# Attention stage of a transformer layer: all four row scalings on VectorE, and two constant loads issued later

## The chip, the cores and the metric

The kernel runs on one Trainium2 chip with all 8 cores, each core on its own eighth of the rows, with no exchange between cores. The metric is the device time in microseconds (us) of the slowest core; the program is one launch.

## The reference

One transformer layer on a sequence of 8192 rows of width 2048, with an unusual attention: for every row, the 16 heads attend to each other, so each softmax is over 16 numbers.

```python
x = x + attn(layernorm(x), w_qkv, w_proj)      # x: 1 x 8192 x 2048
x = x + ffn(layernorm(x), kernel, bias)

def attn(x, w_qkv, w_proj):                    # N_HEAD 16, HEAD_DIM 128
    qkv = (x @ w_qkv.T).reshape(B, N, 3, 16, 128)
    q, k, v = qkv[:, :, 0], qkv[:, :, 1], qkv[:, :, 2]
    att = softmax(einsum('bnid,bnjd->bnij', q, k) * 128 ** -0.5)
    out = einsum('bnij,bnjd->bnid', att, v)    # 16 x 16 per row
    return out.transpose(0, 2, 1, 3).reshape(B, N, 2048) @ w_proj.T

def ffn(x, kernel, bias):                      # 8-bit fake quantization of x, kernel, bias and result
    return fake_quant(relu(fake_quant(x) @ fake_quant(kernel) + fake_quant(bias)))
```

## The kernel before, in words

The kernel is written with raw engine queues: every engine has its own program, runs it strictly in order, and waits on counting semaphores (`wait_ge`) that instructions of other engines raise (`inc`). There is no scheduler; the order in the source is the order on the engine. A core has 1024 rows, and works in stages.

- Stage A: 8 tiles of 128 rows. SyncE (SP) loads `xbuf` (two buffers, 1 MB each; the load of tile t waits for tile t-2), VectorE takes the statistics, ScalarE normalizes into `abuf`, TensorE transposes it with the identity matrix `ident` into PSUM `pH`, ScalarE copies it to `aT`. TensorE's first transpose waits for the semaphore `aCn`, which the loads of `ident` and `mask4` raise. Meanwhile GpSimd (POOL) loads the first three slabs `wqb` of the QKV weights with a cast.
- Stage B: the QKV product, 48 slabs, which leaves `qT`, `kT` and `vT`.
- Stage C: attention, a loop over g of NG = 32 groups. One group is four 128x128 blocks, each of 8 rows times 16 heads, so that a block of q times k holds 8 wanted 16x16 squares on its diagonal; the mask `mask4` keeps those.
- Stage D: the output projection (`wpb` times `sT`), with the residual `xr` and, between its tiles, the quantized FFN weights (`ktb`, `kqb`, `qk`). Then the FFN with its quantization steps, the bias, and the stores.

One pass g of the stage C loop, in the order of each engine's queue (all buffers are in pairs, `g % 2`; k = g - 1):

- TensorE: transpose of v(g) (L317), q times k (g) (L324), transpose of the normalized weights `Abuf`(k) into `pH` (L335), product with v (k) (L344). In short: V(g), QK(g), AT(k), MM(k).
- ScalarE: exponential of group g into `Ebuf` (L358), scaling of blocks 2 and 3 of group g into `Abuf` (L366), copy of the transposed weights `aTTbuf`(k) out of PSUM (L378), copy of the result into `sT` (k) (L383). In short: Exp(g), scale(g), aTT(k), sT(k).
- VectorE: copy of transposed v into `V8buf`(g) (L395), mask (L398), row sums (L401), reciprocal (L405), scaling of blocks 0 and 1 of group g into `Abuf` (L410).
- GpSimd loads one of 16 slabs `wpb` of the projection weights every second pass (L426), into the space that v(g) has left; SyncE loads six of the eight `xr` tiles at the stage's start and two at its end.

The semaphores that matter: `cA8` (QK done), `cExp` (Exp done), `cRcp` (reciprocal done), `cAsc` and `cAsS` (VectorE's and ScalarE's share of the scaling done), `cAtT` (AT done), `cT1e` (aTT done), `cO8` (MM done). A pass g of ScalarE waits for `cA8` of g before Exp, for `cRcp` of g before its scaling, for `cAtT` of k before aTT, and for `cO8` of k before sT.

Of the kernel before, what the change touches and what calls it, by code (L numbers as in the profile page):

```python
# [10 lines left out]
AF = mybir.ActivationFunctionType  # L11
# [15 lines left out]
def build_program():  # L27
# [65 lines left out]
    def S_(name):  # L93
        if name not in sems:
            sems[name] = nc.semaphore(name).__enter__()
            cnt[name] = 0
        return sems[name]

    def inc(instr, name, k=1):
        h = S_(name)  # L100
        instr.then_inc(h, k)
        cnt[name] += k
        return (name, cnt[name])
# [13 lines left out]
    with nc.Block() as blk:  # L117
# [31 lines left out]

        @blk.sync  # L150
        def _(sync):
            inc(sync.dma_start(ident[:, :], d_ident[:, :]), "aCn", 16)
            inc(sync.dma_start(mask4[:, :], d_mask[:, :]), "aCn", 16)
            for t in range(NT):
                if t >= 2:
                    sync.wait_ge(S_("aVn"), t - 1)
                    sync.wait_ge(S_("aVv"), t - 1)
                inc(sync.dma_start(xbuf[t % 2][:, :],
                                   d_xatt[128 * t:128 * (t + 1), :]),
                    f"aLd{t % 2}", 16)  # L160
            for idx in range(2 * NC):
                ft, hh = idx // 2, idx % 2
                if idx >= 2:
                    sync.wait_ge(S_("fK1"), idx - 1)
                inc(sync.dma_start(ktc[idx % 2][:, :],
                                   d_wkT[128 * ft:128 * (ft + 1),
                                         1024 * hh:1024 * (hh + 1)]),
                    f"fKt1{idx % 2}", 16)
# [134 lines left out]
    if PHASES >= 3:  # L303
# [3 lines left out]
     with nc.Block() as blk:  # L307
        @blk.tensor
        def _(tn):
            for g in range(NG + 1):  # L310
                if g < NG:
                    m, cg = g // 2, g % 2
                    if g >= 2:
                        tn.wait_ge(S_("cV8e"), g - 1)
                    for j in range(4):
                        sl = slab(m, 4 * cg + j)
                        tr = tn.transpose(pH[2 + g % 2][:, 128 * j:128 * (j + 1)],  # L317
                                          vT[:, sl:sl + 128], ident[:, :])
                    inc(tr, "cV8t")
                    if g >= 2:  # L320
                        tn.wait_ge(S_("cExp"), g - 1)
                    for j in range(4):
                        sl = slab(m, 4 * cg + j)
                        mm = tn.matmul(pF[g % 2][:, 128 * j:128 * (j + 1)],  # L324
                                       qT[:, sl:sl + 128], kT[:, sl:sl + 128],
                                       start=True, stop=True)
                    inc(mm, "cA8")
                k = g - 1
                if k >= 0:
                    tn.wait_ge(S_("cAsc"), k + 1)  # L330
                    tn.wait_ge(S_("cAsS"), k + 1)
                    if k >= 2:
                        tn.wait_ge(S_("cT1e"), k - 1)
                    for j in range(4):
                        tr = tn.transpose(pH[k % 2][:, 128 * j:128 * (j + 1)],  # L335
                                          Abuf[k % 2][:, 128 * j:128 * (j + 1)],
                                          ident[:, :])
                    inc(tr, "cAtT")
                    tn.wait_ge(S_("cT1e"), k + 1)
                    tn.wait_ge(S_("cV8e"), k + 1)  # L340
                    if k >= 2:
                        tn.wait_ge(S_("cO8e"), k - 1)
                    for j in range(4):
                        mm = tn.matmul(pF[2 + k % 2][:, 128 * j:128 * (j + 1)],  # L344
                                       V8buf[k % 2][:, 128 * j:128 * (j + 1)],
                                       aTTbuf[k % 2][:, 128 * j:128 * (j + 1)],
                                       start=True, stop=True)
                    inc(mm, "cO8")

        @blk.scalar  # L350
        def _(s):
            s.wait_ge(S_("aC12"), 1)
            for g in range(NG + 1):
                if g < NG:
                    s.wait_ge(S_("cA8"), g + 1)
                    if g >= 2:
                        s.wait_ge(S_("cAsc"), g - 1)
                    inc(s.activation(Ebuf[g % 2][:, :], pF[g % 2][:, :], AF.Exp,  # L358
                                     bias=col(80), scale=SCALE), "cExp")

                if g < NG:
                    s.wait_ge(S_("cRcp"), g + 1)
                    if g >= 2:
                        s.wait_ge(S_("cAtT"), g - 1)
                    for j in range(2, 4):
                        instr = s.activation(Abuf[g % 2][:, 128 * j:128 * (j + 1)],  # L366
                                             Embuf[g % 2][:, 128 * j:128 * (j + 1)],
                                             AF.Copy,
                                             scale=C_R4(g % 2)[:, j:j + 1])
                        if j < 3:  # L370
                            inc(instr, "selfS")
                    inc(instr, "cAsS")
                k = g - 1
                if k >= 0:
                    s.wait_ge(S_("cAtT"), k + 1)
                    if k >= 2:
                        s.wait_ge(S_("cO8"), k - 1)
                    inc(s.copy(aTTbuf[k % 2][:, :], pH[k % 2][:, :]), "cT1e")  # L378
                    s.wait_ge(S_("cO8"), k + 1)
                    km, kc = k // 2, k % 2  # L380
                    dst = sT.rearrange("p (t x) -> p t x", t=8)[
                        :, 4 * kc:4 * kc + 4, 128 * km:128 * (km + 1)]
                    inc(s.copy(  # L383
                        dst, pF[2 + k % 2][:, :].rearrange("p (j l) -> p j l", j=4)),
                        "cO8e")

        @blk.vector
        def _(v):
            for g in range(NG + 1):
                if g < NG:  # L390
# [11 lines left out]
                        C_S4(p), Embuf[p][:, :].rearrange("p (b n) -> p b n", b=4),  # L402
                        AX.X), "selfV")
                    wt(v, h_rs)
                    h_rc = inc(v.reciprocal(C_R4(p), C_S4(p)), "cRcp")  # L405
                    if g >= 2:
                        v.wait_ge(S_("cAtT"), g - 1)
                    wt(v, h_rc)
                    for j in range(2):
                        instr = v.tensor_scalar(Abuf[p][:, 128 * j:128 * (j + 1)],  # L410
                                                Embuf[p][:, 128 * j:128 * (j + 1)],
                                                C_R4(p)[:, j:j + 1], None, ALU.mult)
                        if j < 1:
                            inc(instr, "selfV")
                    inc(instr, "cAsc")

# [548 lines left out]
```

## Time and profile before

| | us |
|---|---|
| median of 2 timed runs | 974.39 (973.4 to 975.38) |
| the profiled execution's own time | 972.12 |
| span of its slowest core (core 2), first to last instruction | 970.6 |
| spans of the eight cores | 963.6 to 970.6 |
| mean granted TensorE clock, all cores | 0.842 to 0.845 of full speed |
| TensorE busy, slowest core | 680.5 (70%) |
| VectorE busy | 556.9 (57%) |
| ScalarE busy | 342.9 (35%) |
| stage C, from its first matmul to its last copy (core 2) | 411.46 to 591.17 |

The span is the stretch from the first to the last instruction of a core, so a point in the trace is given in us from its start. The granted clock has two levels, full (1.00, 2.4 GHz) and half (0.50, 1.2 GHz); a mean between them is a mixture in time. Busy shares are over the whole span and mix stages with different limits.

### The profile page before, as it was taken

How to read it: one execution, taken by the hardware profiler on the slowest of the kernel's cores; microseconds unless marked ns; L12 is line 12 of the kernel's file. 1: busy time of each engine (PE TensorE's matmuls, PEld its weight loads, DVE VectorE, ACT ScalarE, POOL GpSimd, SP SyncE). 2: the span in 40 equal slices, each digit the busy share in tenths (PEclk: the TensorE clock that was granted, in tenths of full speed). 3: DMA queues.
4: the chain of work that ended last, by engine and by line, in shares of the span. 5: the costliest groups of instructions: out<-in, count | busy, mean ns of one | idle time of the engine just before them, and what ended most of it. 6: DMA issues, size and time to landing. Idle time of an engine off the chain costs nothing.

```text
span 970.6 us, 11061 instructions; the slowest of 8 cores (963.6 to 970.6 us)
## 1 busy us (share of the span) xinstructions
PE 680.5 (70%) x3524; PEld 341.7 (35%) x3584; DVE 556.9 (57%) x885; ACT 342.9 (35%) x427; POOL 111.0 (11%) x93
## 2 busy tenths in 40 slices
PE   1157999999999999823333335995596645978790
PEld 1033444444444444423223222452052322434340
DVE  2352445454545453443433432898188897899997
ACT  3365434343434343444444441321021233243220
POOL 1000111111111111000000000001200000111324
PEclk9997999999999999955555556997598877999896
DMA  9454799999999978291111114447912210111122
GB/s 163 126 174 43 74 109 146 159 143 153 150 145 162 155 88 81 22 282 23 27 28 23 22 23 141 133 128 176 150 66 88 79 52 1 44 44 44 44 87 87
DMA packets 116985, 94.21 MB, mean 97 GB/s; under 512 B 101184, under 2 KB 101312, under 8 KB 113856
## 3 DMA queue, kind: packets, MB, share of 16 engines
q0 software_dynamic: 103680, 33.56, 34.4%
q1 hardware_dynamic: 13248, 59.94, 18.5%
q8 instruction: 30, 0.49, 0.2%
q14 instruction: 27, 0.22, 0.1%
HBM read 118.65 MB, written 8.39 MB: 131 GB/s over the span
## 4 chain that ended last, share of the span: by engine, by line
DVE 25%; issue 11%; PE 9%; ACT 6%; DMA 5%; DVEq 1%; ACTq 0%; POOLq 0%; POOL 0%; SPq 0%
DMA wpb<-wpT 3%; PE pF L550 3%; DVE cols L401 2%; ACT Ebuf L358 2%; DVE bnbuf L603 2%; PE pF L344 2%; DVE ktb L700 2%; DVE cols L668 2%; DVE xr L569 2%; DVE kti L704 2%; ACT aTTbuf L378 2%; DMA ktb<-wkT 2%; DVE ttile L811 2%; ACT Abuf L366 1%; DVE Embuf L398 1%
## 5 line engine op out<-in xcount | busy, mean ns | idle before, releaser
L288 PE MATMUL pF<-aT,wqb 128*128 128x512 bf16 x736 | 278.9, 379 | 1.6
L286 PE MATMUL pF<-aT,wqb 128*128 128x512 bf16 x706 | 267.6, 379 | 1.0 <-DMA wqb<-wqkvT 1.0
L550 PE MATMUL pF<-qk,xqs 128*128 128x512 bf16 x500 | 116.3, 392 | 4.8 <-ACT xqs L897 3.9
L514 PE MATMUL pF<-wpb,sT 128*128 128x512 bf16 x240 | 99.0, 412 | 22.5 <-DMA wpb<-wpT 20.7
L517 PE MATMUL pF<-wpb,sT 128*128 128x512 bf16 x256 | 105.8, 413 | 4.1 <-DMA wpb<-wpT 1.9
L286 PEld LDWEIGHTS pF<-aT,wqb 128*128 128x128 bf16 x736 | 72.0, 98 | 88.2 <-issue 1.5
L288 PEld LDWEIGHTS pF<-aT,wqb 128*128 128x128 bf16 x736 | 72.0, 98 | 86.7
L344 PE MATMUL pF<-aTTbuf,V8buf 128*128 128x128 bf16 x128 | 18.7, 301 | 115.7 <-ACT aTTbuf L378 115.7
L301 POOL DMA_DIRECT2D wqb<-wqkvT x48 | 55.0, 1146 | 333.9 <-PE pF L288 243.0
L113 DVE CAST qT<-pF 128x512 bf16<-128x512 f32 x16 | 42.9, 2682 | 65.0 <-PE pF L288 50.0
L113 DVE CAST vT<-pF 128x512 bf16<-128x512 f32 x16 | 42.6, 2661 | 58.8 <-PE pF L288 58.8
L550 PEld LDWEIGHTS pF<-qk,xqs 128*128 128x128 bf16 x512 | 51.4, 101 | 67.1 <-issue 11.9
L113 DVE CAST kT<-pF 128x512 bf16<-128x512 f32 x16 | 43.0, 2687 | 50.2 <-PE pF L288 50.2
L114 ACT COPY qk<-pH 128x512 bf16<-128x512 bf16 x64 | 33.5, 592 | 101.9 <-PE pH L493 101.9
L114 ACT CAST kT<-pF 128x512 bf16<-128x512 f32 x16 | 43.2, 2703 | 68.5 <-PE pF L288 68.5
L114 ACT CAST qT<-pF 128x512 bf16<-128x512 f32 x16 | 43.3, 2708 | 66.3 <-PE pF L288 58.7
L114 ACT CAST vT<-pF 128x512 bf16<-128x512 f32 x16 | 42.8, 2672 | 67.7 <-PE pF L288 67.7
L437 POOL TENSOR_TENSOR xr<-xr,junkG 128x2048 f32<-128x2048 f32 x7 | 33.3, 4750 | 223.8 <-DVE junkG L837 223.8
L344 PEld LDWEIGHTS pF<-aTTbuf,V8buf 128*128 128x128 bf16 x128 | 11.2, 127 | 123.2 <-issue 123.2
L395 DVE COPY V8buf<-pH 128x512 bf16<-128x512 bf16 x32 | 13.6, 425 | 70.7 <-PE pH L317 70.7
L266 PE MATMUL pH<-ident,abuf 128*128 128x128 bf16 x128 | 15.2, 290 | 55.3 <-ACT aT L114 36.6
L514 PEld LDWEIGHTS pF<-wpb,sT 128*128 128x128 bf16 x256 | 26.3, 103 | 69.6 <-issue 45.5
(117 smaller groups left out, 875.9 us busy)
## 6 DMA issues: line engine op xcount, KB each, us to landing
wqb<-wqkvT POOLq DMA_DIRECT2D x48, 512.0 KB, 8.0
ktc<-wkT SPq DMA_DIRECT2D x32, 512.0 KB, 7.1
ktb<-wkT SPq DMA_DIRECT2D x32, 512.0 KB, 4.0
xbuf<-x_att SPq DMA_DIRECT2D x8, 1024.0 KB, 7.1
xr<-x_res SPq DMA_DIRECT2D x8, 1024.0 KB, 6.7
wpb<-wpT POOLq DMA_DIRECT2D x32, 256.0 KB, 5.5
out<-xr SPq DMA_DIRECT2D x7, 1024.0 KB, 3.8
bias_b<-bias SPq DMA_DIRECT2D x1, 1024.0 KB, 4.2
```

Of the source, the lines that this page charges most:

```text
L113: return eng.tensor_copy(dst, srcap)
L114: return eng.copy(dst, srcap)
L286: tn.matmul(pa[:, :], wch, aT[:, 1024 * c:1024 * c + 512], start=st, stop=sp)
L288: mm = tn.matmul(pb[:, :], wch, aT[:, 1024 * c + 512:1024 * c + 1024], start=st, stop=sp)
L301: inc(g.dma_start(dst, src), f"bWq{e % 3}", 16)
L344: mm = tn.matmul(pF[2 + k % 2][:, 128 * j:128 * (j + 1)], V8buf[k % 2][:, 128 * j:128 * (j + 1)], aTTbuf[k % 2][:, 128 * j:128 * (j + 1)], ...
L358: inc(s.activation(Ebuf[g % 2][:, :], pF[g % 2][:, :], AF.Exp, bias=col(80), scale=SCALE), "cExp")
L378: inc(s.copy(aTTbuf[k % 2][:, :], pH[k % 2][:, :]), "cT1e")
L437: inc(g.tensor_tensor(xr[:, 2048 * k:2048 * (k + 1)], xr[:, 2048 * k:2048 * (k + 1)], junkG2[:, :], ALU.add), "gOutR")
L514: tn.matmul(pF[2 * (idx % 2)][:, :], lhs, wpb[:, 1024 * m:1024 * m + 512], start=st, stop=sp)
L517: mm = tn.matmul(pF[2 * (idx % 2) + 1][:, :], lhs, wpb[:, 1024 * m + 512:1024 * (m + 1)], start=st, stop=sp)
L550: mm = tn.matmul(pF[u][:, :], xqs[Mt % 2][:, 128 * c:128 * (c + 1)], qk[:, 2048 * c + 512 * u:2048 * c + 512 * (u + 1)], start=(c == 0), s ...
```

## The change

Two edits. In stage C, ScalarE no longer scales blocks 2 and 3; VectorE scales all four, the semaphore `cAsS` is gone, and the reciprocal no longer raises `cRcp` for ScalarE. In stage A, the loads of `ident` and `mask4` are issued on SyncE behind the first two `xbuf` loads instead of ahead of them.

```diff
--- before.py
+++ after.py
@@ -149,9 +149,10 @@
 
         @blk.sync
         def _(sync):
-            inc(sync.dma_start(ident[:, :], d_ident[:, :]), "aCn", 16)
-            inc(sync.dma_start(mask4[:, :], d_mask[:, :]), "aCn", 16)
             for t in range(NT):
+                if t == 2:
+                    inc(sync.dma_start(ident[:, :], d_ident[:, :]), "aCn", 16)
+                    inc(sync.dma_start(mask4[:, :], d_mask[:, :]), "aCn", 16)
                 if t >= 2:
                     sync.wait_ge(S_("aVn"), t - 1)
                     sync.wait_ge(S_("aVv"), t - 1)
@@ -328,7 +329,6 @@
                 k = g - 1
                 if k >= 0:
                     tn.wait_ge(S_("cAsc"), k + 1)
-                    tn.wait_ge(S_("cAsS"), k + 1)
                     if k >= 2:
                         tn.wait_ge(S_("cT1e"), k - 1)
                     for j in range(4):
@@ -358,18 +358,6 @@
                     inc(s.activation(Ebuf[g % 2][:, :], pF[g % 2][:, :], AF.Exp,
                                      bias=col(80), scale=SCALE), "cExp")
 
-                if g < NG:
-                    s.wait_ge(S_("cRcp"), g + 1)
-                    if g >= 2:
-                        s.wait_ge(S_("cAtT"), g - 1)
-                    for j in range(2, 4):
-                        instr = s.activation(Abuf[g % 2][:, 128 * j:128 * (j + 1)],
-                                             Embuf[g % 2][:, 128 * j:128 * (j + 1)],
-                                             AF.Copy,
-                                             scale=C_R4(g % 2)[:, j:j + 1])
-                        if j < 3:
-                            inc(instr, "selfS")
-                    inc(instr, "cAsS")
                 k = g - 1
                 if k >= 0:
                     s.wait_ge(S_("cAtT"), k + 1)
@@ -402,15 +390,15 @@
                         C_S4(p), Embuf[p][:, :].rearrange("p (b n) -> p b n", b=4),
                         AX.X), "selfV")
                     wt(v, h_rs)
-                    h_rc = inc(v.reciprocal(C_R4(p), C_S4(p)), "cRcp")
+                    h_rc = inc(v.reciprocal(C_R4(p), C_S4(p)), "selfV")
                     if g >= 2:
                         v.wait_ge(S_("cAtT"), g - 1)
                     wt(v, h_rc)
-                    for j in range(2):
+                    for j in range(4):
                         instr = v.tensor_scalar(Abuf[p][:, 128 * j:128 * (j + 1)],
                                                 Embuf[p][:, 128 * j:128 * (j + 1)],
                                                 C_R4(p)[:, j:j + 1], None, ALU.mult)
-                        if j < 1:
+                        if j < 3:
                             inc(instr, "selfV")
                     inc(instr, "cAsc")
 
```

How it stands in the queues. ScalarE in the stage C loop, one pass and the start of the next, before (`Ebuf`, `Abuf`, `aTTbuf` as above, the number behind a name tells the two buffers apart):

```order
L358 ACTIVATE Ebuf_71<-pF,cols 128x512 [waits cA8,cAsc]
L366 ACTIVATE Abuf_75<-Embuf_73,cols 128x128 [waits cRcp,cAtT]
L366 ACTIVATE Abuf_75<-Embuf_73,cols 128x128
L378 COPY aTTbuf_76<-pH 128x512 [waits cAtT,cO8]
L383 CAST sT<-pF 128x4x128 [waits cO8]
L358 ACTIVATE Ebuf_70<-pF,cols 128x512 [waits cA8,cAsc]
```

and after (behind the removed block the line numbers of the changed file are lower by 12):

```order
L371 CAST sT<-pF 128x4x128 [waits cO8]
L358 ACTIVATE Ebuf_71<-pF,cols 128x512 [waits cA8,cAsc]
L366 COPY aTTbuf_76<-pH 128x512 [waits cAtT,cO8]
L371 CAST sT<-pF 128x4x128 [waits cO8]
L358 ACTIVATE Ebuf_70<-pF,cols 128x512 [waits cA8,cAsc]
```

The copy aTT(k) now follows Exp(g) directly, and ScalarE's queue has no wait for a result of VectorE's pass g.

VectorE in the same loop, before:

```order
L395 COPY V8buf_78<-pH 128x512 [waits cV8t,cO8]
L398 TENSOR_TENSOR Embuf_72<-Ebuf_70,mask_90 128x512 [waits cExp]
L401 TENSOR_REDUCE cols<-Embuf_72 128x4 [waits selfV]
L405 RECIPROCAL cols<-cols 128x4 [waits selfV]
L410 TENSOR_SCALAR Abuf_74<-Embuf_72,cols 128x128 [waits cAtT,cRcp]
L410 TENSOR_SCALAR Abuf_74<-Embuf_72,cols 128x128
```

and after:

```order
L383 COPY V8buf_78<-pH 128x512 [waits cV8t,cO8]
L386 TENSOR_TENSOR Embuf_72<-Ebuf_70,mask_90 128x512 [waits cExp]
L389 TENSOR_REDUCE cols<-Embuf_72 128x4 [waits selfV]
L393 RECIPROCAL cols<-cols 128x4 [waits selfV]
L398 TENSOR_SCALAR Abuf_74<-Embuf_72,cols 128x128 [waits cAtT,selfV]
L398 TENSOR_SCALAR Abuf_74<-Embuf_72,cols 128x128 x3
```

Two scalings of 128x128 have become four; nothing else is reordered on VectorE.

## Rows read from the trace of the kernel before

**Rows 1.** The chain that ended last, 405 to 600 us, shares by line.

```profile
by line: issue 17.2%; DVE cols L401 11.4%; ACT Ebuf L358 11.4%; PE pF L344 9.6%; ACT aTTbuf L378 7.9%; ACT Abuf L366 7.3%; DVE Embuf L398 7.2%; PE pF L324 6.9%; PE pH L317 6.8%; DMA ktb<-wkT 5.6%; DVE cols L405 3.1%; DVEq L106 0.7%; ACT L35
```

**Rows 2.** Timeline of a stage C pass: start us, us, engine, line, [idle before <-releaser].

```profile
565.26 0.58 PE L344 MATMUL pF<-aTTbuf,V8buf 128*128 128x128 bf16 x4 [3.68 <-ACT aTTbuf L378]
...
565.64 0.63 PE L317 MATMUL pH<-ident,vT 128*128 128x128 bf16 x4
...
566.06 0.63 PE L324 MATMUL pF<-kT,qT 128*128 128x128 bf16 x4
...
566.49 0.63 PE L335 MATMUL pH<-ident,Abuf 128*128 128x128 bf16 x4
566.85 0.69 ACT L358 ACTIVATE Ebuf<-pF,cols 128x512 bf16<-128x512 f32 x1 [0.33 <-PE pF L324]
567.64 0.42 DVE L398 TENSOR_TENSOR Embuf<-Ebuf,mask 128x512 bf16<-128x512 bf16 x1 [0.77 <-ACT Ebuf L358]
568.17 0.69 DVE L401 TENSOR_REDUCE cols<-Embuf 128x4 f32<-128x512 bf16 x1
568.96 0.18 DVE L405 RECIPROCAL cols<-cols 128x4 f32<-128x4 f32 x1
569.24 0.42 DVE L410 TENSOR_SCALAR Abuf<-Embuf,cols 128x128 bf16<-128x128 bf16 x2
569.28 0.69 ACT L366 ACTIVATE Abuf<-Embuf,cols 128x128 bf16<-128x128 bf16 x2 [1.75 <-DVE cols L405]
569.88 0.56 ACT L378 COPY aTTbuf<-pH 128x512 bf16<-128x512 bf16 x1
...
570.80 0.58 PE L344 MATMUL pF<-aTTbuf,V8buf 128*128 128x128 bf16 x4 [3.68 <-ACT aTTbuf L378]
```

**Rows 3.** Windows view, 29 passes from Exp(2) to Exp(31).

```profile
core 2: us, PE busy (x) PEld busy (x) DVE busy (x) ACT busy (x) POOL busy (x), PEclk, DMA share, GB/s
421.80:583.84 162.04, 54.10 (x467) 47.23 (x465) 61.82 (x175) 70.65 (x146) 7.41 (x14) 0.50 0.22 49
```

**Rows 4.** Tile view of Abuf, VectorE's scalings: min/median/max ns.

```profile
L410 DVE TENSOR_SCALAR Abuf<-Embuf,cols x64: 246/252/255, 415.8 to 586.4; 128x128 bf16<-128x128 bf16 x64
```

**Rows 5.** Timeline of the end of stage C.

```profile
583.84 0.69 ACT L358 ACTIVATE Ebuf<-pF,cols 128x512 bf16<-128x512 f32 x1 [0.33 <-PE pF L324]
...
588.17 0.63 PE L335 MATMUL pH<-ident,Abuf 128*128 128x128 bf16 x4
...
588.95 0.59 ACT L378 COPY aTTbuf<-pH 128x512 bf16<-128x512 bf16 x1
...
590.58 0.59 ACT L383 CAST sT<-pF 128x512 bf16<-128x512 f32 x1 [1.03 <-PE pF L344]
```

**Rows 6.** Timeline of the start of stage C.

```profile
411.46 0.38 PE L317 MATMUL pH<-ident,vT 128*128 128x128 bf16 x4 [3.07 <-PEq L117]
...
411.68 0.39 PE L324 MATMUL pF<-kT,qT 128*128 128x128 bf16 x4
...
413.45 0.69 ACT L358 ACTIVATE Ebuf<-pF,cols 128x512 bf16<-128x512 f32 x1
```

**Rows 7.** Timeline, GpSimd's last slab load of stage C.

```profile
583.86 0.53 POOL L426 DMA_DIRECT2D wpb<-wpT  x1 [10.92 <-PE pH L317]
```

**Rows 8.** Page, DMA issues: count, KB each, median us to landing.

```profile
wpb<-wpT POOLq DMA_DIRECT2D x32, 256.0 KB, 5.5
```

**Rows 9.** Windows view of TensorE alone: length, busy (count), granted clock, DMA share, GB/s.

```profile
692.00:698.00 6.00, 3.67 (x7) 0.50 1.05 173
```

**Rows 10.** Timeline of stage A: first loads, first transposes, third tile's statistics.

```profile
1.07 0.38 SPq L152 DMA_DIRECT2D ident<-ident  x1
...
1.98 59.07 SPq L158 DMA_DIRECT2D xbuf<-x_att  x8
...
18.72 1.87 PE L266 MATMUL pH<-ident,abuf 128*128 128x128 bf16 x16 [18.72 <-ACT abuf L196]
...
34.08 2.47 DVE L211 BATCH_NORM_STATS2 bnbuf<-xbuf 128x6 f32<-128x512 f32 x4 [16.17 <-DMA xbuf<-x_att]
```

## The prediction

> **What bounds the kernel now.** I read the chain that ended last first. Over the attention stage it runs through every engine in turn: exponential, row sums, product with v, transposed copy, scaling, mask [rows 1]. No engine is full there: in 162.04 us TensorE is busy 54.10, VectorE 61.82, ScalarE 70.65 [rows 3]. So the stage is bound by waiting, and I read one pass of the timeline [rows 2]. In it I call the pass's group g and the one before it k.
>
> The pass is one closed ring. Exp(g) starts at 566.85. The mask follows at 567.64 (+0.79), the row sums at 568.17 (+0.53), the reciprocal at 568.96 (+0.79). ScalarE's scaling starts at 569.28 (+0.32). The copy aTT(k) starts at 569.88 (+0.60), and MM(k) at 570.80 (+0.92). From MM to the next transpose of v is 0.38, from there to QK 0.42, from QK to Exp 0.79 (565.26, 565.64, 566.06, 566.85). The sum is 5.54, the period of an undisturbed pass [rows 2]. The 29 passes from 421.80 to 583.84 average 5.59, so some are late, by 1.4 us together [rows 3].
>
> What the reader is to see is the place of aTT(k). Its input comes from AT(k), which starts at 566.49 and takes 0.63, so it is there before 567.2. Its engine is idle: ScalarE waits 1.75 us for the reciprocal ahead of its scaling [rows 2]. The copy of the old group stands in ScalarE's queue behind the scaling of the new one, and so TensorE's MM(k), idle for 3.68, and everything behind MM(k), hangs on the softmax of g. The ring closes once a pass although the buffers are in pairs.
>
> **The change part by part.** *ScalarE's queue.* Two scalings leave it (0.69 us for both, 569.28), and with them its wait for the reciprocal. aTT(k) now stands right behind Exp(g). Two rings are left, and the longer one sets the period.
>
> Ring one closes in one pass: Exp(g), aTT(k) 0.60 later (the 0.69 of Exp less the overlap seen between 569.28 and 569.88), MM(k) +0.92, V +0.38, QK +0.42, Exp +0.79: 3.11 us.
>
> Ring two goes through the softmax and closes in two passes, because AT(g) and MM(g) stand one pass later in TensorE's queue, ahead of QK(g+2): Exp(g) to mask 0.79, sums 0.53, reciprocal 0.79, VectorE's scaling 0.28 (568.96 to 569.24), four scalings, hand-over to AT(g), AT to aTT 0.78 (588.17 to 588.95 [rows 5]), MM 0.92, V 0.38, QK 0.42, Exp 0.79. All but two terms are rows.
>
> *The four scalings.* Two take 0.42 together [rows 2] and one 0.252 [rows 4], so each further one adds 0.17, and four take 0.42 + 0.34 = 0.76. If they did not overlap it would be 1.01. I take 0.76, since the row with two shows the overlap.
>
> There the Trainium skill speaks against the change: "VectorE: DVE Perf Modes", § The DRAIN you can't avoid, has the next VectorE operation start only when the pipe is empty. By it the four would take 1.01, which is 0.125 us more a pass. The row with two in 0.42 [rows 2] disagrees, and I stay with it.
>
> *The hand-over from VectorE to TensorE* isn't in the trace as a wait that ends last. The nearest rows are QK's end at 566.06 + 0.63 = 566.69 to Exp at 566.85, which is 0.16 with two semaphores waited for, as AT now has; below, 0.11 inside VectorE (567.64 + 0.42 to 568.17); above, 0.36 from the copy's end to MM (569.88 + 0.56 to 570.80) with three semaphores [rows 2]. I take 0.16, the nearest in kind, and keep 0.11 and 0.36.
>
> Ring two: 0.79 + 0.53 + 0.79 + 0.28 + 0.76 + 0.16 + 0.78 + 0.92 + 0.38 + 0.42 + 0.79 = 6.60 for two passes, 3.30 a pass. It is the longer one. VectorE's own work is no ring above it: 61.82 / 29 = 2.13 a pass now, 2.47 with two more scalings, and gaps of 0.10 between dependent instructions bring it to about 2.7. ScalarE's is 0.69 + 0.56 + 0.59 = 1.84.
>
> *The stage.* Exp(0) starts at 413.45, after a table load that stays [rows 6]. Exp(1) is free at once. Exp(2) needs one round of ring two: 413.45 + 6.60 = 420.05. Exp(31) is 29 passes later: + 95.7 = 515.75. From there to the end: 0.79 + 0.53 + 0.79 + 0.28 + 0.76 + 0.16 + 0.78 = 4.09 to the last aTT, and from it to the end of the last copy what the trace has, 588.95 to 591.17, 2.22 [rows 5]. End at 522.06 in place of 591.17: 69.1 saved. The late passes' 1.4 us may stay: 67.7.
>
> *What starts earlier.* GpSimd loads a slab every second pass, then every 6.6 us, against 5.5 to landing [rows 8]. The last one is issued at 583.86, as Exp(31) starts, and would land 5.5 later, 0.8 us before the new stage's end (6.31 after Exp(31)); the projection uses it as the last of its sixteen slabs. Nothing is late. The other loads at the stage's end and all behind them hang on the stage's own last copy and move with it, so I book the whole gain.
>
> *The two constant loads.* The first `xbuf` load is issued 0.91 us earlier (1.98 against 1.07) [rows 10]. `ident` and `mask4` come behind 2 MB, but TensorE needs them only at 18.72. If they are later, the price is small up to 34.08, when the third tile arrives and ends a wait of 16.17 [rows 10]: the first two tiles' transposes have that gap as cover, and beyond it each us costs one. That third load is issued when tile 0 is normalized, so it can gain up to 0.9, or nothing if the traffic of GpSimd's three slabs sets its landing. The bounds are a gain of 0.9 and a loss of 2; I take a gain of 0.5.
>
> *The sum.* 67.7 + 0.5 = 68.2 off the profiled execution's 972.12 gives 903.9. That execution is 2.3 below the median of the timed runs, 974.39; off the median it gives 906.2.
>
> **The rivals.**
>
> *TensorE's clock rises in the stage.* It runs at half speed, 0.50, through all of it [rows 3]. At full speed four matmuls take 0.39 in place of 0.63 and the next group follows after 0.22 in place of 0.42 [rows 6, 2]. Ring two has QK to Exp and AT to aTT (0.24 less each), V to QK (0.20) and MM to V (0.16) in it: 5.76, or 2.88 a pass, 12.2 us less over 29 passes, 0.84 in the first round and 0.4 in the tail. The projection behind it would open at full speed; I allow up to 3 for that, which no row here prices. 16 in all: 890. For it: TensorE's busy share goes from 54.10 / 162.04 to about 1.87 / 3.30, 57%. Against it: the stretch at 692 has it busy 3.67 of 6 us, 61%, and stays at 0.50 [rows 9]. The Trainium skill ("TensorE: Matmul & The Clock Gate", § What's actually happening) says that the default is the throttled state and that activity releases it; which side 57% in short bursts falls on, no row settles.
>
> *VectorE becomes uneven.* Its work goes from 38% to some 75% of a pass, and GpSimd issues its loads beside it. With scalings that don't overlap (+0.125 a pass), a hand-over of 0.36 (+0.10) and GpSimd's 16 issues of 0.53 [rows 7] each holding VectorE on the ring (8.5 us), it is 31 x 0.225 = 7.0 and 8.5, 15 more: 921. For it: 1.4 us of late passes exist now [rows 3], and my ring has no slack in VectorE. "SBUF — State Buffer", § Who interferes with whom, in the Trainium skill, lets a GpSimd access and a VectorE operation in a two-port mode block each other, whichever comes first. The trace agrees at most to the size of those 1.4 us.
>
> *The change does not do what it says*: something else that I overlooked holds aTT(k) or MM(k) until pass g is through, and the period stays near 5.5. Against it: the queue behind Exp(g) holds only waits for `cAtT` and `cO8`, both long met. 972.
>
> *Slower.* One mechanism: the scalings on VectorE, now with nothing between them, each cost far more than alone. VectorE's own pass of about 2.7 us would then become the bound. To reach the old 5.59 both added ones must cost 1.45 more, some 1.6 each; a loss of 2% (19.5 us, 0.6 a pass) needs 1.9 each, in place of 0.17: 994. The 64 scalings now lie between 0.246 and 0.255 [rows 4].
>
> **How the numbers follow.** The forecast at the half clock: 66%, 906, by itself 901 to 914. The clock rises, wholly or in parts: 18%, 888 to 900. VectorE uneven: 13%, 914 to 922. No effect: 2%. Slower: 1%. The range of 8 in 10 has to take in most of the second and third: 888 to 920. A measurement of this kernel can tell 2% (19.5 us) from no change; all three leading cases are beyond it: faster 0.97, the same 0.02, slower 0.01.
>
> **What would show it.** In the changed kernel's trace: Exp to Exp in pairs that average 3.30; aTT(k) starting behind Exp(g) or 0.78 behind AT(k), not behind the reciprocal; TensorE's wait ahead of MM(k) down from 3.68 to about 1; four scalings in 0.76; the clock at 0.50; the stage from 411 to 522; the stages behind it with their old lengths. I am wrong if the period lies outside 3.1 to 3.6, if the clock rises, or if a later stage takes back what this one gives, a wait for slabs first of all.

## The result, and the profile after

The changed kernel takes 909.53 us (median of 9 runs) where the kernel before, timed beside it, takes 975.42 (8 runs). The ratio is 0.932, with a 95% interval of 0.9297 to 0.9343: 6.8% faster. The forecast was 906, the range 888 to 920. The profiled execution took 905.0 us in all; its slowest core is core 6 with a span of 903.5. The runs of this kernel spread from 905.0 to 912.2 us, apart from one disturbed execution (974.91, with four cores at a lower clock), which the median of 9 holds (it is 909.25 without it) and the ratio leaves out, as do the times, ratios and profiles of the experiments below with theirs.

First the place. The table has medians over the eight cores of each kernel's profiled execution: the first statistics of stage A (start of the first L211), the first matmul of stage B's main loop (L286), stage C from the start of its first matmul (L317) to the end of its last copy (L383), and from there to the end of the core's span (line numbers of the kernel before).

| us | before | after |
|---|---|---|
| first statistics of stage A | 9.4 | 7.2 |
| main loop of stage B begins | 87.0 | 86.7 |
| stage C begins | 408.0 | 407.6 |
| stage C, length | 180.1 | 112.5 |
| end of stage C to end of span | 378.8 | 379.2 |

Stage C gives 67.6 us, and nothing behind it takes that back or adds to it. The first statistics of stage A come 2.2 us earlier; at the later boundaries the lead is 0.3 or 0.4, which is no more than the difference between two kernels that are alike up to there (stage B begins at 87.0 before, and at 86.5 with the scaling edit alone).

The timeline of one double pass of stage C after the change, core 6 (start us, us, engine, line, [idle before <-releaser]); it answers to [rows 2]. Lines from the removed block on are lower by 12 than before: the copy aTT is now L366, the row sums L389, the scalings L398. Between the moved loads and AT they are higher by one (V is L318, QK L325); AT, MM and Exp keep L335, L344 and L358.

```profile
462.72 0.69 ACT L358 ACTIVATE Ebuf<-pF,cols 128x512 bf16<-128x512 f32 x1 [0.33 <-PE pF L325]
463.31 0.59 ACT L366 COPY aTTbuf<-pH 128x512 bf16<-128x512 bf16 x1
463.51 0.43 DVE L386 TENSOR_TENSOR Embuf<-Ebuf,mask 128x512 bf16<-128x512 bf16 x1 [0.77 <-ACT Ebuf L358]
464.04 0.69 DVE L389 TENSOR_REDUCE cols<-Embuf 128x4 f32<-128x512 bf16 x1
...
464.25 0.58 PE L344 MATMUL pF<-aTTbuf,V8buf 128*128 128x128 bf16 x4 [1.09 <-ACT aTTbuf L366]
...
464.83 0.18 DVE L393 RECIPROCAL cols<-cols 128x4 f32<-128x4 f32 x1
...
465.12 0.74 DVE L398 TENSOR_SCALAR Abuf<-Embuf,cols 128x128 bf16<-128x128 bf16 x4
...
465.84 0.69 ACT L358 ACTIVATE Ebuf<-pF,cols 128x512 bf16<-128x512 f32 x1 [0.33 <-PE pF L325]
...
466.11 0.58 PE L335 MATMUL pH<-ident,Abuf 128*128 128x128 bf16 x4 [0.42 <-DVE Abuf L398]
...
466.84 0.59 ACT L366 COPY aTTbuf<-pH 128x512 bf16<-128x512 bf16 x1 [0.31 <-PE pH L335]
...
467.78 0.59 PE L344 MATMUL pF<-aTTbuf,V8buf 128*128 128x128 bf16 x4 [1.09 <-ACT aTTbuf L366]
...
469.38 0.69 ACT L358 ACTIVATE Ebuf<-pF,cols 128x512 bf16<-128x512 f32 x1 [0.33 <-PE pF L325]
```

What to see: the copy aTT(k) (463.31) starts 0.59 us behind Exp (462.72), with no wait; before, it stood 3.03 us behind (566.85 to 569.88 [rows 2]). The next Exp comes 3.12 us after the first, the one after that 3.54 later (465.84, 469.38). This alternation is the mark of a ring that closes once in two passes: the softmax of the group that begins at 462.72 runs through mask, sums, reciprocal and four scalings to AT at 466.11, aTT at 466.84 and MM at 467.78, and only from there to the Exp at 469.38, that is 6.66 us in all. The MM at 464.25 between them belongs to the group before. The four scalings take 0.74 together (465.12), so they overlap as two did.

The windows view of the 29 passes from Exp(2) to Exp(31), which answers to [rows 3]:

```profile
core 6: us, PE busy (x) PEld busy (x) DVE busy (x) ACT busy (x) POOL busy (x), PEclk, DMA share, GB/s
422.34:519.90 97.56, 58.19 (x465) 44.69 (x464) 69.63 (x233) 52.80 (x88) 7.44 (x14) 0.50 0.40 83
```

97.56 us in place of 162.04, 3.36 a pass in place of 5.59. VectorE is now busy for 69.63 of it, 71% in place of 38%; the clock is 0.50 as before.

The end of stage C, which answers to [rows 5] and [rows 7]:

```profile
519.90 0.69 ACT L358 ACTIVATE Ebuf<-pF,cols 128x512 bf16<-128x512 f32 x1 [0.33 <-PE pF L325]
519.92 0.53 POOL L414 DMA_DIRECT2D wpb<-wpT  x1 [6.12 <-PE pH L318]
...
524.02 0.59 ACT L366 COPY aTTbuf<-pH 128x512 bf16<-128x512 bf16 x1 [1.28 <-PE pH L335]
...
525.63 0.59 ACT L371 CAST sT<-pF 128x512 bf16<-128x512 f32 x1 [1.03 <-PE pF L344]
```

The last slab load is issued with the last Exp (519.92), 6.3 us before the stage ends (525.63 + 0.59 = 526.22). The tail from Exp(31) is 526.22 - 519.90 = 6.32; it was forecast as 6.31.

Stage A, which answers to [rows 10]:

```profile
1.07 0.85 SPq L159 DMA_DIRECT2D xbuf<-x_att  x2
...
1.96 0.42 SPq L154 DMA_DIRECT2D ident<-ident  x1
2.43 1.15 SPq L155 DMA_DIRECT2D mask<-mask  x1
8.20 2.47 DVE L212 BATCH_NORM_STATS2 bnbuf<-xbuf 128x6 f32<-128x512 f32 x4 [8.20 <-DMA xbuf<-x_att]
...
17.24 1.86 PE L267 MATMUL pH<-ident,abuf 128*128 128x128 bf16 x16 [17.24 <-ACT abuf L197]
...
32.59 2.47 DVE L212 BATCH_NORM_STATS2 bnbuf<-xbuf 128x6 f32<-128x512 f32 x4 [16.15 <-DMA xbuf<-x_att]
```

The first `xbuf` loads are issued at 1.07, and the first statistics start at 8.20 on this core. The constants behind them are there at 17.24, when TensorE has its first input; it waits for `abuf`, not for them. But the third tile comes at 32.59 where it came at 34.08 [rows 10], on the slowest cores of each; over eight cores the median lead is 2.2 us at the first tile, 0.7 at the third (33.2 and 32.5) and 0.4 where stage B begins, which is no longer more than two like kernels differ there.

### The profile page after: what moved, and what is told of

Read it like the earlier page. It is cut to its first block, busy times and chain, and to the rows that moved or that the text cites. A ratio compares the mean times of both kernels' runs of the same rounds, so it can differ in the third digit from the quotient of the medians.

```text
span 903.5 us, 11027 instructions; the slowest of 8 cores (896.3 to 903.5 us)
## 1 busy us (share of the span) xinstructions
PE 690.0 (76%) x3584; PEld 339.0 (38%) x3584; DVE 565.6 (63%) x949; ACT 323.0 (36%) x363; POOL 110.9 (12%) x93
## 4 chain that ended last, share of the span: by engine, by line
DVE 24%; PE 12%; issue 9%; DMA 5%; ACT 3%; DVEq 1%; POOLq 0%; POOL 0%; ACTq 0%; SPq 0%
DMA wpb<-wpT 4%; PE pF L502 3%; PE pF L505 3%; DVE bnbuf L591 2%; DVE cols L656 2%; DVE ttile L799 2%; PE pF L538 2%; DVE cols L802 2%; ACT Ebuf L358 1%; DVE cols L389 1%; DVE ktb L688 1%; DVE Abuf L398 1%; DVE xr L557 1%; ACT aTTbuf L366 1%; PE pF L344 1%
## 5 line engine op out<-in xcount | busy, mean ns | idle before, releaser
L287 PE MATMUL pF<-aT,wqb 128*128 128x512 bf16 x736 | 279.9, 380 | 3.1 <-DMA wqb<-wqkvT 3.1
L289 PE MATMUL pF<-aT,wqb 128*128 128x512 bf16 x736 | 280.0, 380 | 0.0
L502 PE MATMUL pF<-wpb,sT 128*128 128x512 bf16 x256 | 106.0, 414 | 24.0 <-DMA wpb<-wpT 21.8
L538 PE MATMUL pF<-qk,xqs 128*128 128x512 bf16 x512 | 117.7, 393 | 3.6 <-ACT xqs L885 3.6
L505 PE MATMUL pF<-wpb,sT 128*128 128x512 bf16 x256 | 106.2, 415 | 0.0
L425 POOL TENSOR_TENSOR xr<-xr,junkG 128x2048 f32<-128x2048 f32 x7 | 33.2, 4749 | 223.6 <-DVE junkG L825 223.6
L344 PE MATMUL pF<-aTTbuf,V8buf 128*128 128x128 bf16 x128 | 18.7, 301 | 35.5 <-ACT aTTbuf L366 35.5
L212 DVE BATCH_NORM_STATS2 bnbuf<-xbuf 128x6 f32<-128x512 f32 x32 | 19.8, 681 | 37.8 <-DMA xbuf<-x_att 37.8
L856 ACT CAST qx<-xi 128x2048 bf16<-128x2048 int32 x8 | 15.2, 1903 | 65.9 <-DVE xi L640 65.9
```

The source lines that it names most:

```text
L212: h_bn = inc(v.bn_stats(bnbuf[:, 6 * q4:6 * q4 + 6], xbt[:, 512 * q4:512 * (q4 + 1)]), "selfV")
L287: tn.matmul(pa[:, :], wch, aT[:, 1024 * c:1024 * c + 512], start=st, stop=sp)
L289: mm = tn.matmul(pb[:, :], wch, aT[:, 1024 * c + 512:1024 * c + 1024], start=st, stop=sp)
L344: mm = tn.matmul(pF[2 + k % 2][:, 128 * j:128 * (j + 1)], V8buf[k % 2][:, 128 * j:128 * (j + 1)], aTTbuf[k % 2][:, 128 * j:128 * (j + 1)], ...
L425: inc(g.tensor_tensor(xr[:, 2048 * k:2048 * (k + 1)], xr[:, 2048 * k:2048 * (k + 1)], junkG2[:, :], ALU.add), "gOutR")
L502: tn.matmul(pF[2 * (idx % 2)][:, :], lhs, wpb[:, 1024 * m:1024 * m + 512], start=st, stop=sp)
```

## The experiments

Ten kernels ran, each as a diff to the changed kernel or the kernel before. The ratio is to the kernel before on the same chip, with its 95% interval; period is the mean from Exp(2) to Exp(31), clock the granted clock in that stretch; all but the ratio are medians over the eight cores of the profiled execution.

| kernel | ratio | period | stage C | clock in C | end of C to end |
|---|---|---|---|---|---|
| before | 1 | 5.60 | 180.1 | 0.50 | 378.8 |
| changed | 0.932 (0.9297 to 0.9343) | 3.36 | 112.5 | 0.50 | 379.2 |
| scaling edit alone | 0.9292 (0.9267 to 0.9318) | 3.36 | 112.4 | 0.50 | 378.9 |
| constants edit alone | 0.9987 (0.9967 to 1.0007) | 5.60 | 180.1 | 0.50 | 379.1 |
| ScalarE scales, last in its queue | 0.9423 (0.94 to 0.9446) | 3.81 | 126.2 | 0.50 | 378.4 |
| ScalarE scales, between aTT and sT | 0.9324 (0.927 to 0.9377) | 3.55 | 117.7 | 0.50 | 379.5 |
| wait for the reciprocal kept | 0.9822 (0.9795 to 0.9848) | 5.03 | 162.5 | 0.50 | 379.1 |
| eight scalings | 0.9408 (0.9369 to 0.9446) | 3.69 | 122.9 | 0.50 | 379.1 |
| filler matmuls | 0.9162 (0.91 to 0.9225) | 2.92 | 99.2 | 0.98 | 377.8 |
| two groups deep | 0.9238 (0.9134 to 0.9342) | 3.11 | 103.6 | 0.50 | 378.7 |
| two deep and filler | 0.9064 (0.9019 to 0.9108) | 2.60 | 88.8 | 0.98 | 378.1 |
| those, and ScalarE shares, a group late | 0.9014 (0.8913 to 0.9114) | 2.54 | 85.9 | 0.97 | 378.7 |

The last column is the control: no edit of stage C changes what lies behind it by more than 1.4 us, and the eight cores of the changed kernel alone spread there from 377.2 to 381.5. So stage C's length can be read for each kernel without the noise of the whole time. It is the better measure here: most times of the experiments lie some us below expectations that were counted from the changed kernel's 909.5 (the scaling edit alone by 5, with the same stage C), and no run shows why. The ratios of the eight scalings, the filler, two deep, and both together rest on three runs of the kernel before, those of the two kernels with ScalarE between and a group late on four.

### The two edits apart

The scaling edit alone:

```diff
+            inc(sync.dma_start(ident[:, :], d_ident[:, :]), "aCn", 16)
+            inc(sync.dma_start(mask4[:, :], d_mask[:, :]), "aCn", 16)
             for t in range(NT):
-                if t == 2:
-                    inc(sync.dma_start(ident[:, :], d_ident[:, :]), "aCn", 16)
-                    inc(sync.dma_start(mask4[:, :], d_mask[:, :]), "aCn", 16)
```

> The changed kernel with the two constant loads put back ahead of the first xbuf load, so the scaling edit alone. Theory (the stage C ring carries the whole gain): stage C stays at 112.5 us against 180.1 before, and the time is that of the changed kernel, 909.5, plus 0 to 1 us. Rival (the earlier xbuf loads, which bring the first statistics forward by some 2 us, carry through to the end): 911 to 912.

The constants edit alone is the other half of the change's diff, on the kernel before.

> The kernel before with only the constant loads moved behind the first two xbuf loads. Theory: 0 to 0.9 us faster than 975.4, so not to be told from no change; the first statistics start 1 to 2 us earlier, and the start of stage B moves by less, since the third tile's landing is set by the traffic. Rival: the 2 us come through whole, 973.4, or the late constants hold up the transposes, over 976.

Measured: 904.12 us, ratio 0.9292, for the scaling edit; 972.67 against 973.65, ratio 0.9987 with 1 inside its interval, for the constants. The first interval overlaps that of the whole change, so the constants edit is worth nothing that these runs can tell, and the scaling edit has the whole gain. The time was expected as 909.5 to 910.5 and came out 5 lower; stage C (112.4) and what lies behind it (378.9) are as in the changed kernel, so the 5 do not come from there. With the constants edit the median first statistics start at 7.3 in place of 9.4, the third tile's at 32.4 in place of 33.2, and stage B at 86.4 in place of 87.0. The first part of the expectation holds: the lead is lost on the way to the third tile. That GpSimd's slab traffic is what it is lost to was only argued.

### Who scales, or where the copy stands

The rival reading of the gain is that ScalarE was relieved, or that VectorE is faster at scaling (0.74 for four against 0.69 for two). The first experiment leaves the work shared as before and only moves ScalarE's block of L361 to L372 in its queue, against the kernel before with the constants edit:

```diff
-                if g < NG:
-                    s.wait_ge(S_("cRcp"), g + 1)
...
-                    inc(instr, "cAsS")
                 k = g - 1
                 if k >= 0:
...
                         "cO8e")
+                if g < NG:
+                    s.wait_ge(S_("cRcp"), g + 1)
...
+                    inc(instr, "cAsS")
```

> ScalarE keeps its two scalings and VectorE its two, but ScalarE's queue has them behind aTT(k) and sT(k): Exp(g), aTT(k), sT(k), scale(g). Theory (the place of aTT(k) in the queue is what counts, not who scales): the two-pass ring is 0.60 + 0.92 + 0.68 + 0.50 + 0.69 + 0.16 + 0.78 + 0.92 + 0.38 + 0.42 + 0.79 = 6.84, 3.42 a pass, some 0.06 more with the late passes as in the changed kernel: stage C 116, time 913. Rival (the gain comes from taking work from ScalarE, or from VectorE's faster scalings): the period stays near 5.5 and the time near 975.

Measured: 917.28, stage C 126.2, a period of 3.81. The order of the queue alone brings 53.9 of the 67.6 us, so who scales is not the main thing. But 3.42 a pass was forecast, and that missed by 0.4. Its timeline (core 1):

```profile
440.76 0.70 ACT L380 ACTIVATE Abuf<-Embuf,cols 128x128 bf16<-128x128 bf16 x2
...
441.36 0.68 ACT L359 ACTIVATE Ebuf<-pF,cols 128x512 bf16<-128x512 f32 x1
...
441.71 0.59 PE L336 MATMUL pH<-ident,Abuf 128*128 128x128 bf16 x4 [0.67 <-ACT Abuf L380]
...
442.44 0.59 ACT L367 COPY aTTbuf<-pH 128x512 bf16<-128x512 bf16 x1 [0.40 <-PE pH L336]
...
443.38 0.59 PE L345 MATMUL pF<-aTTbuf,V8buf 128*128 128x128 bf16 x4 [1.09 <-ACT aTTbuf L367]
...
444.06 0.59 ACT L372 CAST sT<-pF 128x512 bf16<-128x512 f32 x1 [1.03 <-PE pF L345]
...
444.54 0.70 ACT L380 ACTIVATE Abuf<-Embuf,cols 128x128 bf16<-128x128 bf16 x2
```

There is a ring that I had left out. The scaling at 440.76 releases AT at 441.71 (+0.95), that the copy at 442.44 (+0.73), that MM at 443.38 (+0.94), that sT at 444.06 (+0.68), and the next scaling stands behind sT in the queue, at 444.54 (+0.48): 3.78 in one pass. The expectation had taken aTT(k) as ready whenever Exp was through; here it waits for AT(k), because the scaling that feeds AT(k) comes so late.

The next kernel opens that ring, with the scaling between aTT(k) and sT(k):

> As the run with ScalarE's two scalings last, but they stand between aTT(k) and sT(k): Exp(g), aTT(k), scale(g), sT(k). The run with them last had a period of 3.78, from a ring I had left out: scale(g) to AT(g) 0.95, to aTT(g) 0.73, to MM(g) 0.94, to sT(g) 0.68, to scale(g+1) 0.48. Theory (that ring, closed by sT standing ahead of the scaling): here it opens, and the longest is Exp(g) through the softmax to scale(g), sT(k), Exp(g+1): 0.79 + 0.53 + 0.79 + 0.32 + 0.60 + 0.50 = 3.53 a pass, stage C 118 to 120, time 909 to 911. Rival (two engines sharing the scaling cost the 0.4 a pass by themselves): 3.8, 917.

Measured: 910.63, stage C 117.7, and passes of 3.50 each but for a few late ones, mean 3.55; forecast 3.53. The two kernels differ in one place of the queue and share the work alike, so the revised account holds and its rival falls. In time this one can't be told from the changed kernel (0.9324 and 0.932); stage C is 5.2 us longer.

The opposite experiment has VectorE do all the scaling, and puts back only the wait:

```diff
+                if g < NG:
+                    s.wait_ge(S_("cRcp"), g + 1)
                 k = g - 1
                 if k >= 0:
                     s.wait_ge(S_("cAtT"), k + 1)
```

> VectorE scales all four blocks as in the changed kernel, but ScalarE still waits for the reciprocal of group g ahead of aTT(k). Theory: the one-pass ring is closed again, without the 0.60 of the two scalings: 0.79 + 0.53 + 0.79 + 0.32 + 0.92 + 0.38 + 0.42 + 0.79 = 4.94 a pass; 31 x (4.94 - 3.36) = 49 us more than the changed kernel, 958. Rival (who does the work is what counts): near 909.5.

Measured: 955.77, a period of 5.03, stage C 162.5, 49.9 longer than in the changed kernel. One wait with no work behind it takes back 74% of the gain. Core 5's timeline:

```profile
501.11 0.69 ACT L358 ACTIVATE Ebuf<-pF,cols 128x512 bf16<-128x512 f32 x1 [0.33 <-PE pF L325]
...
503.22 0.18 DVE L395 RECIPROCAL cols<-cols 128x4 f32<-128x4 f32 x1
...
503.60 0.59 ACT L368 COPY aTTbuf<-pH 128x512 bf16<-128x512 bf16 x1 [1.80 <-DVE cols L395]
...
504.54 0.59 PE L344 MATMUL pF<-aTTbuf,V8buf 128*128 128x128 bf16 x4 [3.15 <-ACT aTTbuf L368]
...
506.13 0.69 ACT L358 ACTIVATE Ebuf<-pF,cols 128x512 bf16<-128x512 f32 x1 [0.33 <-PE pF L325]
```

The copy (L368) starts 0.38 behind the reciprocal, with 1.80 us of idle ScalarE ahead of it, and Exp comes again after 5.02 us.

### How long the ring is, and how often it closes

Four more scalings on VectorE ahead of the four, into a buffer that nothing reads; the result is unchanged:

```diff
+                    for j in range(4):
+                        inc(v.tensor_scalar(kqb[0][:, 128 * j:128 * (j + 1)],
+                                            Embuf[p][:, 128 * j:128 * (j + 1)],
+                                            C_R4(p)[:, j:j + 1], None, ALU.mult), "selfV")
```

> The changed kernel with four more scalings of 128x128 on VectorE ahead of the four, into a buffer that nothing reads, 4 x 0.17 = 0.68 us a pass. Theory (they lie on a ring that closes once in two passes): half of it shows, 0.34 a pass, 31 x 0.34 = 10.5, time 920, as long as VectorE's own pass (some 2.7 + 0.68 = 3.4) stays under the period of 3.7. Rival (VectorE is the bound, or the ring closes once a pass): the whole 0.68 shows, 21 us, 931.

Measured: a period of 3.69, 0.33 above the changed kernel's 3.36. The timeline (core 1) shows the price of the four: 482.47 to 483.13 is 0.66, and half of that is 0.33. Stage C is 10.4 longer against 10.5 expected; the time is 917.09 against 920.

```profile
482.47 0.74 DVE L398 TENSOR_SCALAR kqb<-Embuf,cols 128x128 bf16<-128x128 bf16 x4
...
483.13 0.74 DVE L403 TENSOR_SCALAR Abuf<-Embuf,cols 128x128 bf16<-128x128 bf16 x4
...
483.78 0.42 DVE L383 COPY V8buf<-pH 128x512 bf16<-128x512 bf16 x1
...
484.12 0.58 PE L335 MATMUL pH<-ident,Abuf 128*128 128x128 bf16 x4 [0.53 <-DVE Abuf L403]
484.54 0.42 DVE L386 TENSOR_TENSOR Embuf<-Ebuf,mask 128x512 bf16<-128x512 bf16 x1 [0.34 <-ACT Ebuf L358]
```

Behind the scalings the copy V8 (483.78) follows at once, and the mask (484.54) still waits 0.34 for Exp: VectorE is nearly full here and still not the bound.

Two groups deep, in the loops of TensorE and ScalarE, so that the softmax has a pass more before AT(k):

```diff
-            for g in range(NG + 1):
+            for g in range(NG + 2):
...
-                k = g - 1
+                k = g - 2
```

> The changed kernel with AT, MM, aTT and sT done for group g - 2 in place of g - 1 in pass g, on TensorE and ScalarE. Theory (ring two is the bound now, ring one of 3.11 is next): ring two closes in three passes and drops out, Exp to Exp is an even 3.11 in place of 3.54 and 3.11 in turn, stage C 3.11 x 31 and one pass more at the end; 0.25 x 31 = 7.8 less and about 2 back: 904. Rival (a one-pass bound on VectorE or ScalarE sets 3.36): no gain, 910 to 913.

Measured: 897.58, stage C 103.6, 8.9 shorter where 7.8 less 2 was expected, a period of 3.11 without the alternation. The expectation had left out the first round: from the first Exp to Exp(2) it now takes 3.2 in place of 6.4. ScalarE on core 4:

```profile
447.57 0.69 ACT L358 ACTIVATE Ebuf<-pF,cols 128x512 bf16<-128x512 f32 x1 [0.33 <-PE pF L325]
448.16 0.58 ACT L366 COPY aTTbuf<-pH 128x512 bf16<-128x512 bf16 x1
449.77 0.59 ACT L371 CAST sT<-pF 128x512 bf16<-128x512 f32 x1 [1.03 <-PE pF L344]
450.69 0.69 ACT L358 ACTIVATE Ebuf<-pF,cols 128x512 bf16<-128x512 f32 x1 [0.33 <-PE pF L325]
```

Exp to Exp is 3.12 (447.57, 450.69). That is ring one as the prediction summed it: 3.11. With ring two out of the way it is the bound, so both rings are shown, 3.11 by this kernel and 6.60 for two passes by the changed one, which has 6.66.

### TensorE's clock

The filler: two matmuls of constants a pass, in TensorE's wait ahead of MM(k), into the tile that MM(k) then overwrites. The result is unchanged.

```diff
                     inc(tr, "cAtT")
+                    if k >= 2:
+                        tn.wait_ge(S_("cO8e"), k - 1)
+                    for _ in range(2):
+                        tn.matmul(pF[2 + k % 2][:, :], ident[:, :], mask4[:, :],
+                                  start=True, stop=True)
                     tn.wait_ge(S_("cT1e"), k + 1)
                     tn.wait_ge(S_("cV8e"), k + 1)
-                    if k >= 2:
-                        tn.wait_ge(S_("cO8e"), k - 1)
```

> The changed kernel with two 128x512 matmuls of constants a pass between AT(k) and MM(k), into the PSUM tile that MM(k) overwrites; they take 0.86 us at the half clock of TensorE's 1.1 us wait there. Theory: they raise the granted clock to 1.00 through stage C, ring two goes from 6.60 to 5.76, 2.88 a pass, and the time falls by 12 to 16 us, to 894 to 898. Rival: the clock stays at 0.50 and the filler costs nothing or up to 0.2 a pass, 909 to 915.

Measured: 891.28 (894 to 898 expected), ratio 0.9162, a period of 2.92 (2.88 expected), stage C 99.2, 13.3 shorter. The windows view of core 7, ten microseconds each:

```profile
core 7: us, PE busy (x) PEld busy (x) DVE busy (x) ACT busy (x) POOL busy (x), PEclk, DMA share, GB/s
410.00:420.00 10.00, 5.00 (x40) 3.31 (x40) 5.51 (x19) 4.86 (x8) 0.55 (x1) 0.66 0.84 215
420.00:430.00 10.00, 5.48 (x64) 3.68 (x65) 8.20 (x29) 5.47 (x11) 1.11 (x2) 1.00 0.96 224
...
440.00:450.00 10.00, 6.95 (x60) 4.24 (x58) 7.35 (x25) 5.85 (x10) 0.53 (x1) 0.83 0.34 53
450.00:460.00 10.00, 5.73 (x66) 3.79 (x66) 8.35 (x30) 5.71 (x11) 1.06 (x2) 1.00 0.32 47
```

The clock is full from 420 us on, but for one fall in the stretch at 440, in which 60 matmuls fit in place of 66. It is full again after it, while TensorE goes on with the same passes. On the eight cores the full clock begins between 413 and 422 us; cores 2 and 6 have a like fall at 436, cores 1, 3 and 4 one or two before 431, and cores 0 and 5 none. The Trainium skill ("TensorE: Matmul & The Clock Gate", § What's actually happening) has activity release the clock; this run agrees, from 0.50 to 0.98 by two matmuls a pass; nothing else was changed but the place of one wait (`cO8e`), which moved ahead of them. Useless work that fits into a wait makes the kernel some 1.7% faster (0.9162 against 0.932).

Both edits together:

> The two edits of the runs before together: two groups deep and the filler. Theory: at the full clock ring one is 0.55 + 0.60 + 0.92 + 0.22 + 0.20 = 2.5, so VectorE's own pass of about 2.75 becomes the bound; stage C about 92, time 888 to 892. Rival: the clock stays at half, as two groups deep alone, 904.

Measured: 882.12 (888 to 892 expected), ratio 0.9064, period 2.60, stage C 88.8 (92 expected). The windows view from Exp(2) on, core 6:

```profile
core 6: us, PE busy (x) PEld busy (x) DVE busy (x) ACT busy (x) POOL busy (x), PEclk, DMA share, GB/s
428.06:493.10 65.04, 41.17 (x450) 25.92 (x450) 56.84 (x201) 45.87 (x77) 6.34 (x12) 1.00 0.56 103
```

VectorE is busy 56.84 of 65.04 us, 87%, and the period of most passes is 2.58. On the same core its instructions follow each other with no wait that the profile shows: the scalings at 460.91, V8 at 461.56, the mask at 461.90, the sums at 462.42, the reciprocal at 463.21, the next scalings at 463.49. So VectorE is the bound now, as forecast, at 2.58 in place of 2.75. Last, ScalarE takes two scalings back, but for group g - 1, between aTT(g - 2) and sT(g - 2); VectorE keeps two, and its mask and TensorE's AT wait for `cAsS`:

```diff
                     inc(s.copy(aTTbuf[k % 2][:, :], pH[k % 2][:, :]), "cT1e")
+                q = g - 1
+                if 0 <= q < NG:
+                    s.wait_ge(S_("cRcp"), q + 1)
+                    if q >= 2:
+                        s.wait_ge(S_("cAtT"), q - 1)
+                    for j in range(2, 4):
...
+                    inc(instr, "cAsS")
+                if k >= 0:
                     s.wait_ge(S_("cO8"), k + 1)
```

> Two groups deep and the filler, and ScalarE takes two of the four scalings back, one group late: Exp(g), aTT(g-2), scale(g-1), sT(g-2); VectorE's mask waits for it. Theory (with those two edits VectorE's own pass of 2.58 is the bound): it falls to some 2.24, and ring one at the full clock, 0.60 + 0.82 + 0.22 + 0.23 + 0.54 = 2.4, takes over; 31 x 0.17 = 5 less, time 879 to 881. Rival (ring one or the clock is already the bound, or the extra waits cost what is gained): 884 to 886.

Measured: 882.94, ratio 0.9014, with an interval that holds the ratio of the kernel before it: not to be told apart in time, and between the forecast (879 to 881) and its rival. Stage C is 85.9, 3.0 shorter, against 5 expected. Its window, core 4:

```profile
core 4: us, PE busy (x) PEld busy (x) DVE busy (x) ACT busy (x) POOL busy (x), PEclk, DMA share, GB/s
425.00:490.00 65.00, 42.37 (x468) 26.95 (x468) 52.95 (x156) 58.70 (x130) 6.88 (x13) 1.00 0.60 117
```

VectorE is down to 52.95 of 65.00, but ScalarE is up to 58.70, 90%: the load has changed sides. Some passes take 2.40, which is the ring one of the forecast, but most others 2.50 to 2.68, for a mean of 2.54. One of these on the same core:

```profile
455.07 0.69 ACT L377 ACTIVATE Abuf<-Embuf,cols 128x128 bf16<-128x128 bf16 x2 [0.27 <-DVE cols L413]
...
455.67 0.56 ACT L389 CAST sT<-pF 128x512 bf16<-128x512 f32 x1
...
456.31 0.69 ACT L362 ACTIVATE Ebuf<-pF,cols 128x512 bf16<-128x512 f32 x1
...
457.77 0.38 PE L348 MATMUL pF<-aTTbuf,V8buf 128*128 128x128 bf16 x4 [0.93 <-ACT aTTbuf L370]
```

ScalarE's scaling waits for the reciprocal, and Exp stands behind it in the queue. That makes a ring which the expectation had left out: from V at 452.83 over V8 (453.10), mask (453.44), sums (453.96), reciprocal (454.75), scaling (455.07), sT (455.67), Exp (456.31), aTT (456.90) and MM (457.77) to V at 457.99, 5.16 in two passes, 2.58 each. It is read from the trace; no run tested it.

## Why the prediction was right

- *The ring through the queue of ScalarE* (5.54 a pass): shown from both sides. Moving the block and nothing else opens it (5.60 to 3.81); putting the wait back and nothing else closes it (3.36 to 5.03, against 4.94 summed from rows).
- *Ring one, 3.11*: the two-deep kernel runs at 3.11.
- *Ring two, 6.60 for two passes*: 6.66 in the trace. The hand-over from VectorE to TensorE, which the prediction took from the nearest row in kind, was taken as 0.16 and is 0.25 (465.12 + 0.74 to 466.11); AT to aTT was taken as 0.78 and is 0.73; the scalings 0.76 and 0.74. That it counts half was shown by the eight scalings (0.66 more on VectorE, 0.33 more a pass).
- *The stage*: 69.1 less 1.4 for late passes, 67.7; measured 67.6. So close a match is partly luck: the ring is 0.03 a pass longer than summed, 0.9 over 29 passes, while the first round takes 6.4 in place of 6.60 and the late passes cost about 1.0 in place of 1.4.
- *The scalings overlap*: 0.74 for four, each 0.249 long. The estimate of 1.01 that was weighed there, from the Trainium skill ("VectorE: DVE Perf Modes", § The DRAIN you can't avoid), does not come out. The prediction had read that section only in part: it also says that a next operation that is not held starts earlier, and this kernel, with a scaling every 0.17 us, agrees with that.
- *The constants*: taken as 0.5 within -0.9 to +2. The edit alone can't be told from nothing. The lead at the start was 2.2 us, more than the 0.91 of the issue times, and the 0.4 at stage B is not more than two like kernels differ there.
- *The stages behind keep their length*: 378.8 and 379.2. No load became late.
- *The rivals.* The clock did not rise by itself: 0.50 on all eight cores. Of its price, 16 us, 13.4 was for stage C (12.2, 0.84 and 0.4), and the filler gives 13.3 there. The up to 3 allowed behind it had no row: 377.8 against 379.2 lies within the spread of the changed kernel's own cores. VectorE became uneven only a little: against the 3.33 of undisturbed double passes ((3.12 + 3.54) / 2) the mean of 3.36 leaves 1 us for late passes, where 1.4 was taken over from the kernel before and 8.5 stood as the bound for GpSimd's issues. The blocking that the Trainium skill ("SBUF — State Buffer", § Who interferes with whom) has between GpSimd and VectorE can be no larger than that 1 us here. The no-effect and the slower case did not come.
- *The sum*: 903.9 for the profiled execution, 905.0 measured; 906 for the median, 909.5 measured. Of the 3.5 us, 1.0 is that the kernel before took 975.42 in these runs and not 974.39; the rest is not in the trace of the profiled execution, which lies at the low end of the timed runs.

## What to carry to other kernels

Where no engine is full, write the ring down, term by term from the rows, and count in how many passes it closes; a term on a ring that closes in two passes counts half. Look in each in-order queue for an instruction that waits for the new group ahead of one that serves the old one: moving the second ahead of the first brought most of this gain, and a single wait put back undid it. Then sum the next ring, since it is where the gain ends (3.30 here, then 3.11, then VectorE's 2.58).

## What the hardware showed that was not expected

- TensorE's clock stayed at 0.50 through stage C in all nine kernels without filler, at passes from 5.60 down to 3.11 us, and was 0.97 to 0.98 in the three with two more 128x512 matmuls a pass: the stage became 13.3 us shorter by added work.
- In the filler kernel the clock fell once to a mean of 0.83 in the stretch from 440 to 450 us on core 7, with the same instructions in each pass as later ones, and with waits of TensorE before it as long as later ones (1.16 us ahead of AT at 439.86, and again at 446.36, where it stayed full). What made it fall is open; in the two kernels with filler that are two groups deep it did not fall before the last Exp once it was full.
- A second 128x128 scaling on VectorE costs 0.17 us behind the first although each is 0.25 long, and ScalarE's Exp followed by a copy costs 0.59 in place of 0.69.
- Loads issued 0.91 us earlier brought the first tile 2.2 us earlier: what they pass on the way counts too. Which part of it is the 160 KB of constants and which GpSimd's three slab loads, issued from 1.57 on, was not tried.
